# First layer's edge sums: one product of 195 columns per block, with the three parts added on VectorE

## The chip, the cores and the metric

The kernel runs on one core of one Trainium2 chip. The metric is the device time of one execution in microseconds (us). Before the change it is 4831.45 us, the median of 3 runs (4831.15 to 4832.38).

## What is computed

Two layers of a graph transformer over 6250 nodes with 256 features. The change lies in the first layer. Its graph convolution sums, for every node, the projected rows of its neighbours (106,250 directed edges with the loops):

```
x = features * norm_src @ W_gcn                 # 64 columns
agg = segment_sum(x[src], dst, num_segments=n)
h = relu(agg * norm_dst + b_gcn)
x = x + (h @ W_out + b_out) + linear_attention(layernorm(x))
x = x + mixture_of_8_experts(layernorm(x))      # two hidden layers of 256, gates by softmax
```

The second layer has a graph attention, another linear attention, and 4 experts with a router that is itself an attention over 131,072 edges.

## The kernel before

The program runs in stages, one after the other, with a barrier between them. The one that the change touches is the stage of the first layer's experts, class `Stage1`, some 490 to 1958 us into the span. It works on two things that don't need each other until the next tile.

**The experts.** The 49 windows of 128 nodes are taken as 7 tiles of 7 windows. In each tile, 8 experts (`e` 0 to 7) follow one another; expert e of tile c is unit 8c + e. For each unit TensorE makes 4 products of the second hidden layer (`layer(c, e, 1, k)`, L1503), 4 of the next expert's first layer (L1503 again), and 4 `last` products (L1516) for pairs of windows. ScalarE takes the hidden layers out of PSUM (L1645). VectorE adds each `last` result, times the gate, to the rows (`weighted`, L1822).

**The edges of the next tile.** The edges are sorted by destination and cut into blocks of 128 edges, each within one window of destinations. Four blocks are a group (`GROUP = 4`); this stage has 187 groups, q = 0 to 186. GpSimd gathers the rows of a group's source nodes by an indirect DMA for each block (L1392, five buffers of groups). A gathered row is the fp32 value of 65 numbers (64 sums and a count) cut into three bf16 parts, 195 columns in all (`PARTS = 3`, `GCOL = 65`). VectorE makes a 0/1 matrix of destinations for a group (`one_hot`, L1717). TensorE's `edges(q)` multiplies it with the rows: for each of 4 blocks three products of 65 columns, added up in PSUM (L1415, 12 in a group). Two PSUM banks take turns (`q % 2`). VectorE's `add_edges` adds each of the 4 results of 65 columns to the row of its window in `acc` (L1732).

**The order is written out by hand**, and each engine works through its own list. A unit has four places ("shares" 0 to 3) for groups of edges. On TensorE: share 0, a sorting step, `layer` products, share 1, a sorting step, `layer` products, share 2, `last` for pairs 0 and 1, share 3, `last` for pairs 2 and 3, and on to share 0 of the next unit. On VectorE: share 0, share 1, share 2, `weighted` for pairs 0 and 1, share 3, `weighted` for pairs 2 and 3. Most shares hold one group; in the first tile eight of them hold two, and in the units e = 7 shares 1 and 2 follow each other on TensorE with nothing between them.

**Two more things are in VectorE's list.** A bitonic sort of the router's edges, for a later stage, is spread over the units (L1096, L1098, L1112). In 5 units of every tile, and in all 8 of the last, a part of it stands between `weighted` for pair 1 and share 3. TensorE's sorting step turns keys (L1079) and waits for that part (L1163). In e = 1 a bias is added in four steps (L1808), and in e = 7 the next tile's rows are normalised (L1782) and turned by TensorE (L1456).

`edges(q)` waits for the 0/1 matrix, for the rows, and for the adds of group q - 2, that is for its bank. GpSimd waits for the products of group q - 5.

Of the kernel before, what the change touches and what calls it, by code (L numbers as in the profile page):

```python
# [10 lines left out]
ALU = mybir.AluOpType  # L11
ACT = mybir.ActivationFunctionType
AXX = mybir.AxisListType.X
ENG = mybir.EngineType

P = 128
# [15 lines left out]
PARTS = 3  # L32
GCOL = GCN + 1
# [18 lines left out]
GROUP = 4  # L52
# [1118 lines left out]
class Stage1:  # L1171
# [83 lines left out]
    def __init__(self, f, nc, R, A):  # L1255
# [39 lines left out]
        self.gt = f.sb("gt", [E0, TPI, P])  # L1295
        self.h1 = f.sb("h1", [P, C, TOK])
        self.h2 = f.sb("h2", [P, C, TOK])
        self.pe = f.ps("pe", [P, 2, 512])
        self.ph = f.ps("ph", [P, 3, 512])
        self.po = f.ps("po", [P, 2, 2, D])  # L1300
# [2 lines left out]
        self.s_c, self.s_st, self.s_bn, self.s_bnr, self.s_scaled, self.s_made, self.s_cnt = (  # L1303
            f.sem(n) for n in ("c", "st", "bn", "bnr", "scaled", "made", "cnt"))
        self.s_rows = [f.sem(f"rows{b}") for b in range(self.ROWS)]
        self.s_hot, self.s_sum, self.s_acc = (f.sem(n) for n in ("hot", "sum", "acc"))
        self.s_xm, self.s_mixed, self.s_side, self.s_sa, self.s_x = (
            f.sem(n) for n in ("xm", "mixed", "side", "sa", "x"))
        self.s_hf, self.s_nd, self.s_ndr, self.s_hr = (f.sem(n) for n in ("hf", "nd", "ndr", "hr"))
# [87 lines left out]
    def tensor(self, t):  # L1397
# [9 lines left out]
        def edges(q):  # L1407
            b = q % self.ROWS
            t.wait_ge(self.s_hot, q + 1)
            t.wait_ge(self.s_rows[b], 16 * GROUP * (q // self.ROWS + 1))  # L1410
            if q >= 2:
                t.wait_ge(self.s_acc, GROUP * (q - 1))
            for u in range(GROUP):
                for k in range(PARTS):
                    mm = t.matmul(self.pe[:, q % 2, u * GCOL:(u + 1) * GCOL], self.hot[:, q % self.HOTS, :, u],  # L1415
                                  self.rows[:, b, u, k * GCOL:(k + 1) * GCOL], start=(k == 0), stop=(k == PARTS - 1))
            mm.then_inc(self.s_sum, 1)

        def mix(n, q):
# [112 lines left out]
        for c in range(ITER):  # L1532
            more = c + 1 < ITER
            for e in range(E0):
                unit = E0 * c + e
                su = self.sorting(c, e)
                for q in self.share(unit, 0):
                    edges(q)
# [8 lines left out]
                for q in self.share(unit, 1):  # L1547
                    edges(q)
# [9 lines left out]
                for q in self.share(unit, 2):  # L1558
                    edges(q)
# [136 lines left out]
    def vector(self, v):  # L1696
# [13 lines left out]
        def one_hot(q):  # L1710
            if q >= self.GROUPS:
                return
            if q >= self.HOTS:
                v.wait_ge(self.s_sum, q - self.HOTS + 1)
            t = GROUP * (self.first() + q)
            dst = R.gdst[:, t:t + GROUP]
            v.tensor_tensor(self.hot[:, q % self.HOTS], self.count[:, :, :],  # L1717
                            dst.unsqueeze(1).to_broadcast([P, P, GROUP]), ALU.is_equal).then_inc(self.s_hot, 1)

        def add_edges(qs):  # L1720
            for q in qs:
                one_hot(q + self.HOTS - 1)
                t = GROUP * (self.first() + q)
                _, ws = self.nc.values_load_multi_w_load_instructions(
                    R.gwin[0:1, t:t + GROUP], engines=(ENG.DVE,), min_val=0, max_val=W - 1,
                    skip_runtime_bounds_check_because="a count of at most W - 1 windows")
                v.wait_ge(self.s_sum, q + 1)
                for u in range(GROUP):
                    if GROUP * q + u:
                        v.wait_ge(self.s_acc, GROUP * q + u)  # L1730
                    aw = self.acc[:, bass.ds(ws[u], 1), :].rearrange("p a d -> p (a d)")
                    v.tensor_tensor(aw, aw, self.pe[:, q % 2, u * GCOL:(u + 1) * GCOL], ALU.add).then_inc(self.s_acc, 1)  # L1732

        def gather_sums(n, done):
            win[n] = self.windows(ENG.DVE, n)
# [114 lines left out]
        for c in range(ITER):  # L1850
            more = c + 1 < ITER
            for e in range(E0):
                unit = E0 * c + e
                su = self.sorting(c, e)
                add_edges(self.share(unit, 0))
                if e == 0:
                    weigh_gates(c)
# [6 lines left out]
                if su is not None:  # L1864
                    self.sort.vector(v, sst, su, 0)
                add_edges(self.share(unit, 1))
                if e == 1:
                    add_bias(c, 1)
# [4 lines left out]
                if su is not None:  # L1873
                    self.sort.vector(v, sst, su, 1)
                add_edges(self.share(unit, 2))
                if e == 1:
                    add_bias(c, 2)
# [1373 lines left out]
```

## Time and profile before

| | |
|---|---|
| median of 3 runs | 4831.45 us |
| profiled execution | 4826.72 us, of which its span is 4825.0 us |
| PE, busy | 3819.0 us, 79% of the span |
| DVE, busy | 3259.6 us, 68% |
| ACT, busy | 2202.3 us, 46% |
| POOL, busy | 2816.7 us, 58% |

PE is TensorE's matmuls, PEld its weight loads, DVE VectorE, ACT ScalarE, POOL GpSimd. A row of a timeline gives the start in us from the start of the span, the duration, the engine, the line, the operation, what it writes and reads, and its shape. x12 at its end means twelve of a kind in a row. A bracket behind it is the engine's idle time ahead of it and what ended that. The rows of other views end with the busy time, the mean ns of one, and the idle time before them.

### The profile page before, as it was taken

The page shows a single profiled execution, that of the slowest core. Times are in us where ns is not written, and L with a number is a line of the kernel's source. Part 1 is how long each engine was busy: PE and PEld are TensorE (multiplying, and loading weights), DVE is VectorE, ACT ScalarE, POOL GpSimd, SP SyncE. Part 2 cuts the span into 40 slices and gives each one's busy share as a digit, 9 for nine tenths or more (in the row PEclk, how much of TensorE's full clock was granted, in tenths as well). Part 3 has the DMA queues.
Part 4 walks back from the last instruction along what each step waited for, and adds up shares of the span by engine and source line. Part 5 has one row for each costly group of instructions (what it writes and reads, how often), then busy time and mean ns, then how long its engine had stood idle before and what let it go on. Part 6 is the DMA issues. An engine that isn't in the chain of part 4 may idle for free. (4 is left out here: it accounts for less than half of the span.)

```text
span 4825.0 us, 68016 instructions
## 1 busy us (share of the span) xinstructions
PE 3819.0 (79%) x17730; PEld 2381.1 (49%) x17730; DVE 3259.6 (68%) x10150; ACT 2202.3 (46%) x3971; POOL 2816.7 (58%) x2922
## 2 busy tenths in 40 slices
PE   7478789999999999768888888764448888878776
PEld 6344456656665566534444444443424444444444
DVE  7667274645546455488888888876566777777777
ACT  4123222233323223356666666620346666666665
POOL 0355376656656420077777777730477777777775
PEclk9999799999999999989999999886568889998888
DMA  1232311111111100344444444531222222222221
GB/s 60 54 88 64 99 46 34 42 34 37 41 30 40 23 16 1 126 125 138 140 137 136 139 140 140 138 91 32 64 34 39 40 40 44 41 39 40 39 38 28
DMA packets 277159, 323.15 MB, mean 67 GB/s; under 512 B 78502, under 2 KB 232004, under 8 KB 276796
## 3 DMA queue, kind: packets, MB, share of 16 engines
q0 software_dynamic: 105328, 175.77, 16.5%
q1 hardware_dynamic: 171468, 143.20, 10.1%
q8 instruction: 147, 2.41, 0.2%
q14 instruction: 216, 1.77, 0.1%
HBM read 288.85 MB, written 29.89 MB: 66 GB/s over the span
## 5 line engine op out<-in xcount | busy, mean ns | idle before, releaser
L2716 POOL DMA_INDIRECT st_rows<-tabr,router_rsrc x1072 | 1022.2, 954 | 334.7 <-issue 322.1
L1392 POOL DMA_INDIRECT st_rows<-tab,graph_gsrc x748 | 741.8, 992 | 499.8 <-PE st_pe L1415 299.0
L2134 POOL DMA_INDIRECT all_XT<-tab,graph_gsrc x880 | 867.6, 986 | 272.2 <-issue 252.5
L1645 ACT ACTIVATE st_h<-st_ph,st_shift,st_scale 128x448 f32<-128x448 f32 x448 | 324.4, 724 | 757.4 <-PE st_ph L1503 757.2
L2164 PE MATMUL st_po<-all_XT,st_hot 128*128 128x264 f32 x1760 | 579.6, 457 | 84.2 <-DVE gat_sum L2317 83.0
L2317 DVE TENSOR_TENSOR gat_sum<-gat_sum,st_po 128x264 f32 x880 | 376.5, 428 | 143.5 <-DVE gat_sum L2317 75.4
L2164 PEld LDWEIGHTS st_po<-all_XT,st_hot 128*128 128x128 f32 x1760 | 297.5, 204 | 288.1 <-DVE gat_sum L2317 176.3
L2761 PE MATMUL st_px<-all_XT,st_w 128*128 128x512 f32 (+1 forms) x832 | 424.0, 659 | 10.7 <-ACT st_hid L2821 10.7
L1732 DVE TENSOR_TENSOR gcn_acc<-gcn_acc,st_pe 128x65 f32 x748 | 166.3, 222 | 381.7 <-PE st_pe L1415 290.7
L2773 PE MATMUL st_py<-st_w,st_hid 128*128 128x256 f32 x1568 | 422.5, 416 | 0.5 <-ACT st_hid L2821 0.5
L2734 PE MATMUL st_pad<-st_adr,st_hott 128*128 x1072 | 121.1, 183 | 346.4 <-DVE st_zd L2887 325.4
L1516 PE MATMUL st_po<-all_XT,st_h 128*128 128x256 f32 x1568 | 366.7, 385 | 13.5 <-DVE all_X L1822 9.9
L1503 PE MATMUL st_ph<-st_h,all_XT 128*128 128x448 f32 x896 | 363.3, 557 | 3.3 <-ACT st_h L1645 3.3
L1503 PE MATMUL st_ph<-st_xt,all_XT 128*128 128x448 f32 x896 | 361.8, 558 | 0.0
L2773 PEld LDWEIGHTS st_py<-st_w,st_hid 128*128 128x128 f32 x1568 | 305.3, 205 | 44.8 <-ACT st_hid L2821 0.9
L1516 PEld LDWEIGHTS st_po<-all_XT,st_h 128*128 128x128 f32 x1568 | 292.5, 191 | 67.6 <-issue 14.1
L2734 PEld LDWEIGHTS st_pad<-st_adr,st_hott 128*128 128x128 bf16 x1072 | 87.1, 98 | 453.8 <-issue 433.0
L2923 DVE TENSOR_TENSOR router_racc<-router_racc,st_po 128x60 f32 x1072 | 229.8, 214 | 119.9 <-DVE router_racc L2923 6.8
L2810 ACT ACTIVATE st_rows<-st_d 128x16 f32<-128x16 f32 x268 | 57.9, 216 | 509.4 <-DVE st_d L2897 508.4
L2308 DVE TENSOR_TENSOR all_XT<-all_XT,st_wps 128x1024 f32<-128x1024 f32 x220 | 266.8, 1213 | 0.5 <-ACT all_XT L2233 0.5
L1822 DVE SCALAR_TENSOR_TENSOR all_X<-st_po,st_gate,all_X 128x256 f32 x392 | 168.4, 477 | 141.8 <-PE st_po L1516 128.0
L2761 PEld LDWEIGHTS st_px<-all_XT,st_w 128*128 128x128 f32 x832 | 170.9, 222 | 186.2 <-issue 175.2
(489 smaller groups left out, 7233.4 us busy)
## 6 DMA issues: line engine op xcount, KB each, us to landing
st_bc<-drowr SPq DMA_DIRECT2D x268, 128.0 KB
st_bc<-drow SPq DMA_DIRECT2D x220, 128.0 KB
st_rows<-tabr,router_rsrc POOLq DMA_INDIRECT x1072
all_XT<-tab,graph_gsrc POOLq DMA_INDIRECT x880
xtd<-tab_xt SPq DMA_DIRECT2D x98, 128.0 KB, 1.9
st_rows<-tab,graph_gsrc POOLq DMA_INDIRECT x748
tab<-gat_sum SPq DMA_DIRECT2D x7, 924.0 KB
all_XT<-xtd SPq DMA_DIRECT2D x49, 128.0 KB
```

The costliest lines, as they stand in the source:

```text
L1392: g.indirect_dma_start(self.rows[:, b, u, :], None, self.R.tab0, bass.IndirectOffsetOnAxis(self.R.gsrc[:, t:t + 1], 0)).then_inc(self.s_ro ...
L1503: mm = t.matmul(self.ph[:, m % 3, 0:HALF], (self.w1, self.w2)[l][:, e, i, fb * P:(fb + 1) * P], src[:, i, h * HALF:(h + 1) * HALF], start= ...
L1516: mm = t.matmul(self.po[:, q % 2, j - 2 * k, :], self.h2[:, i, j * P:(j + 1) * P], self.wo[:, e, i, :], start=(i == 0), stop=(i == C - 1))
L1645: a.activation((self.h1, self.h2)[l][:, fb, h * HALF:(h + 1) * HALF], self.ph[:, m % 3, 0:HALF], ACT.Relu, bias=self.shift[:, l, i:i + 1], ...
L2134: g.indirect_dma_start(self.rows[:, b, u, :], None, self.R.tab1, bass.IndirectOffsetOnAxis(self.R.gsrc[:, t:t + 1], 0)).then_inc(self.s_ro ...
L2164: t.matmul(self.po[:, m % self.BANKS, 0:GROW], self.hot[:, q % self.HOTF, u], self.rows[:, q % self.ROWS, u, :], start=True, stop=True).th ...
L2308: v.tensor_tensor(m, m, self.wps[:, :, :].unsqueeze(3).to_broadcast([P, GROUP, GH, GC]), ALU.mult)\
L2317: v.tensor_tensor(aw, aw, self.po[:, (GROUP * q + u) % self.BANKS, 0:GROW], ALU.add).then_inc(self.s_acc, 1)
L2716: g.indirect_dma_start(self.rows[:, b, u, :], None, self.R.tabr, bass.IndirectOffsetOnAxis(self.R.rsrc[:, t:t + 1], 0)).then_inc(self.s_ro ...
L2761: mm = t.matmul(self.px[:, i, 0:n * P], self.w1[:, e, c, fb * P:(fb + 1) * P], R.XT[:, c, r * P:(r + n) * P], start=(c == 0), stop=(c == C ...
L2773: t.matmul(self.py[:, m % 2, 0:D], self.hid[:, (E1 * u + e) % 2, fb, j * P:(j + 1) * P], self.w2[:, e, fb, :], start=(fb == 0), stop=False)
L2923: v.tensor_tensor(aw, aw, self.po[:, q % self.SUMB, u * n:(u + 1) * n], ALU.add).then_inc(self.s_acc, 1)
```

## The change

Each block's product is now one of 195 columns instead of three of 65. A block's result takes 195 columns of PSUM, two blocks fill 390 of a bank's 512, and a group fills both banks. So the banks no longer take turns: `edges(q)` waits until the results of group q - 1 have been read. VectorE adds the three parts of each result by two reductions per group (one for each bank), into a new tile `es` in SBUF, and the four adds to `acc` read that tile.

```
+        self.es = f.sb("es", [P, GROUP, GCOL])
@@ edges(q)
-            if q >= 2:
-                t.wait_ge(self.s_acc, GROUP * (q - 1))
+            if q:
+                t.wait_ge(self.s_es, 2 * q)
+            n = PARTS * GCOL
             for u in range(GROUP):
-                for k in range(PARTS):
-                    mm = t.matmul(self.pe[:, q % 2, u * GCOL:(u + 1) * GCOL], self.hot[:, q % self.HOTS, :, u],
-                                  self.rows[:, b, u, k * GCOL:(k + 1) * GCOL], start=(k == 0), stop=(k == PARTS - 1))
+                mm = t.matmul(self.pe[:, u // 2, u % 2 * n:(u % 2 + 1) * n], self.hot[:, q % self.HOTS, :, u],
+                              self.rows[:, b, u, 0:n], start=(u % 2 == 0), stop=False, skip_group_check=True)
             mm.then_inc(self.s_sum, 1)
@@ add_edges(qs)
                 v.wait_ge(self.s_sum, q + 1)
+                if q:
+                    v.wait_ge(self.s_acc, GROUP * q)
+                for h in range(2):
+                    v.tensor_reduce(self.es[:, 2 * h:2 * h + 2, :],
+                                    self.pe[:, h, 0:2 * PARTS * GCOL].rearrange("p (u k d) -> p u d k", u=2, k=PARTS),
+                                    AXX, ALU.add).then_inc(self.s_es, 1)
                 for u in range(GROUP):
+                    v.wait_ge(self.s_es, 2 * q + u // 2 + 1)
                     if GROUP * q + u:
                         v.wait_ge(self.s_acc, GROUP * q + u)
                     aw = self.acc[:, bass.ds(ws[u], 1), :].rearrange("p a d -> p (a d)")
-                    v.tensor_tensor(aw, aw, self.pe[:, q % 2, u * GCOL:(u + 1) * GCOL], ALU.add).then_inc(self.s_acc, 1)
+                    v.tensor_tensor(aw, aw, self.es[:, u, :], ALU.add).then_inc(self.s_acc, 1)
```

## Rows read from the trace of the kernel before

**Rows 1.** The page's part 2: busy tenths and granted clock in 40 slices.

```profile
PE   7478789999999999768888888764448888878776
DVE  7667274645546455488888888876566777777777
PEclk9999799999999999989999999886568889998888
```

**Rows 2.** Windows: us, busy time (x instructions) of each engine, clock, DMA.

```profile
560.00:1760.00 1200.00, 1121.44 (x5818) 732.29 (x5817) 658.88 (x1907) 350.38 (x501) 722.77 (x728) 0.98 0.15 36
```

**Rows 3.** Groups by line, 560 to 1760 us.

```profile
L1732 DVE TENSOR_TENSOR gcn_acc<-gcn_acc,st_pe 128x65 f32 x748 | 166.3, 222 | 381.7 <-PE st_pe L1415 290.7 <-issue 7.6 <-DVE gcn_acc L1732 3.9
L1415 PE MATMUL st_pe<-st_rows,st_hot 128*128 128x65 bf16 x2244 | 103.1, 196 | 11.4 <-DVE gcn_acc L1732 7.9 <-DMA st_rows<-tab,graph_gsrc 2.4 <-issue 1.2
```

**Rows 4.** Timeline of PE in a unit with sorting (shares 2, 3 and 0).

```profile
1100.63 0.56 PE L1415 MATMUL st_pe<-st_rows,st_hot 128*128 128x65 bf16 x12
1101.03 3.70 PE L1516 MATMUL st_po<-all_XT,st_h 128*128 128x256 f32 x16
1104.56 0.56 PE L1415 MATMUL st_pe<-st_rows,st_hot 128*128 128x65 bf16 x12
1107.63 0.56 PE L1415 MATMUL st_pe<-st_rows,st_hot 128*128 128x65 bf16 x12
1109.17 0.63 PE L1079 MATMUL st_side<-all_ident,st_skey 128*128 128x128 f32 x4 [0.98 <-DVEq L1163]
1109.63 6.18 PE L1503 MATMUL st_ph<-st_h,all_XT 128*128 128x448 f32 x16
```

**Rows 5.** Timeline of DVE in the same stretch.

```profile
1102.57 0.68 DVE L1096 TENSOR_TENSOR st_skey<-st_skey 128x512 f32<-128x512 f32 x1
1103.17 0.68 DVE L1098 TENSOR_TENSOR st_skey<-st_skey 128x512 f32<-128x512 f32 x1
1109.70 1.33 DVE L1732 TENSOR_TENSOR gcn_acc<-gcn_acc,st_pe 128x65 f32 x4 [0.17 <-issue]
```

**Rows 6.** Timeline of PE: two bf16 rows of another stage, 256 columns wide.

```profile
4390.80 0.28 PE L2775 MATMUL st_py<-router_b2p,st_ones 3*128 3x256 bf16 x1
4391.01 1.35 PE L2773 MATMUL st_py<-st_w,st_hid 128*128 128x256 f32 x5
```

**Rows 7.** Groups by line, DVE: the later stages' sums of three parts.

```profile
L2290 DVE TENSOR_REDUCE st_zd<-st_pad 128x64 f32<-128x192 f32 x220 | 77.1, 351 | 15.8 <-issue 15.2 <-PE st_pad L2152 0.4
L2887 DVE TENSOR_REDUCE st_zd<-st_pad 128x32 f32<-128x96 f32 x268 | 69.0, 257 | 63.2 <-issue 59.8 <-PE st_pad L2734 3.4
```

**Rows 8.** Timelines of PE and DVE at share 0, first and last late case.

```profile
837.25 0.56 PE L1415 MATMUL st_pe<-st_rows,st_hot 128*128 128x65 bf16 x12
...
837.78 1.32 DVE L1732 TENSOR_TENSOR gcn_acc<-gcn_acc,st_pe 128x65 f32 x4 [0.17 <-issue]
...
1734.24 0.56 PE L1415 MATMUL st_pe<-st_rows,st_hot 128*128 128x65 bf16 x12
...
1735.53 1.32 DVE L1732 TENSOR_TENSOR gcn_acc<-gcn_acc,st_pe 128x65 f32 x4 [0.17 <-issue]
```

**Rows 9.** Timelines of PE and DVE at a share with two groups, first tile.

```profile
635.69 0.96 PE L1415 MATMUL st_pe<-st_rows,st_hot 128*128 128x65 bf16 x24
642.39 0.56 PE L1415 MATMUL st_pe<-st_rows,st_hot 128*128 128x65 bf16 x12 [2.61 <-DVE gcn_acc L1732]
642.79 7.95 PE L1503 MATMUL st_ph<-st_h,all_XT 128*128 128x448 f32 x16
...
640.93 1.32 DVE L1732 TENSOR_TENSOR gcn_acc<-gcn_acc,st_pe 128x65 f32 x4 [0.17 <-issue]
```

**Rows 10.** Timeline of PE: places that already wait for DVE behind its edge adds.

```profile
1029.31 1.77 PE L1425 MATMUL st_side<-st_xm,all_weff 128*128 128x448 f32 x4 [1.13 <-DVE all_X L1808]
...
1172.19 1.06 PE L1456 MATMUL st_side<-all_ident,st_xn 128*128 128x128 f32 x4 [2.50 <-DVE st_xn L1782]
...
1179.49 0.63 PE L1456 MATMUL st_side<-all_ident,st_xn 128*128 128x128 f32 x4 [0.63 <-DVE st_xn L1782]
```

More of the change, by code:

```diff
@@ L1305, in __init__ @@
         self.s_rows = [f.sem(f"rows{b}") for b in range(self.ROWS)]
-        self.s_hot, self.s_sum, self.s_acc = (f.sem(n) for n in ("hot", "sum", "acc"))
+        self.s_hot, self.s_sum, self.s_acc, self.s_es = (f.sem(n) for n in ("hot", "sum", "acc", "es"))
         self.s_xm, self.s_mixed, self.s_side, self.s_sa, self.s_x = (
```

## The prediction, made before the changed kernel was run

> **What bounds the kernel now.** I read the page's slices first. In slices 5 to 16, where the experts of the first layer run, PE stands at 9 tenths or nearly so while DVE stands at 4 to 6, and the granted clock is almost full [rows 1]. The windows view says it in numbers: from 560 to 1760 us, the stretch with edges, PE is busy for 1121 of 1200 us, DVE for 659 [rows 2]. So TensorE bounds this stage, and only 79 us of it are PE's idle time. The stages before and after don't change and follow behind barriers, so what the stage gains or loses the kernel gains or loses. Then the groups by line: the adds of the edges sit behind 291 us of DVE idling for the products, while PE idled only 7.9 us for those adds [rows 3]. VectorE has time on average. The question is whether it has it where TensorE will now wait, and that only the timelines of both engines side by side can tell.
>
> **The product of 195 columns.** A group of 12 products of 65 columns holds PE for 0.40 us: the next work starts 1101.03 - 1100.63 us after it [rows 4], and 24 in a row take 0.96 us against 0.56 for 12 [rows 9]. That is 33 ns for each. The trace has no bf16 product of 128 rows and 195 columns. From below: 16 products of 448 columns in fp32 take 6.18 us, some 375 ns from start to start once the tail of the last is off [rows 4]; taken as two passes over 448 columns that is 0.42 ns per column, so 82 ns for 195 and 0.33 us for a group, 0.07 less than now. From above: the bf16 product of 256 columns is followed 0.21 us later [rows 6], 0.16 us scaled to 195, 0.64 a group, 0.24 more than now. I take 0.07 less, since 65 columns at 33 ns (0.5 ns a column) already lie near the lower price. Over 187 groups that is **-13 us**; the ends are -13 and +45.
>
> The Trainium skill (TensorE: Matmul & The Clock Gate, section Back-to-back issue gap) gives for a stream of weight load and matmul about 81 ns at 128 columns and 131 at 512. Read off between them, as an estimate, 195 columns take 90 ns, and the term would be -7 us instead of -13; the 33 ns measured here at 65 columns lies far under the page's 81.
>
> **The two reductions.** The same kind of sum over three parts from PSUM is in the later stages: 351 ns for 192 elements, 257 for 96 [rows 7], so 0.98 ns an element, and 351 + 198 x 0.98 = 545 ns for 390. Two of a kind that don't depend on each other overlap by 0.08 us (0.68 long, 0.60 apart) [rows 5]: both are done 1.01 us after the first starts, and the first add can start after 0.95. The adds of 65 columns now read SBUF instead of PSUM. I leave them at 222 ns [rows 3]: bounds are 0 and 50 ns gained, the adds being chained by their semaphore (4 in 1.33 us [rows 5], 0.11 between two). So each group costs DVE **0.95 us more**, 178 us in all. DVE then is busy for 837 of some 1300 us, and is still not the bound by its sum. Where DVE idles for a product that costs nothing. The new waits ahead of each add are met before the previous add has ended; nothing.
>
> **The wait that changes.** `edges(q)` waited for the adds of q-2, and now waits for the reductions of q-1. What is queued behind it on TensorE is all the rest: the `last` and `layer` products. The new wait ends 1.01 us plus a semaphore after the moment at which the adds of q-1 start now; between the end of four adds and the start of the PE work that waited for it lie 642.39 - 642.25 = 0.14 us [rows 9]. I used 1.1 us and went through the timelines of all 187 groups: start of L1732 of q-1, plus 1.1, minus start of L1415 of q. In 145 of 186 cases it is negative, mostly by 2 to 7 us, since one `layer` or `last` block lies between. In 41 it is positive, 109 us in all:
> - share 0 of a unit that follows a sorting part: 21 cases of 1.0 to 5.1 us, 61.5 in all. The unit of [rows 4, 5] shows why: PE reaches share 0 at 1107.63, VectorE is in the sort and comes to share 3's adds at 1109.70, so 3.2 us are missing. The first case is 837.78 + 1.1 - 837.25 = 1.6, the last 1735.53 + 1.1 - 1734.24 = 2.4 [rows 8].
> - the first tile, with two groups in a share: 14 cases, 40.2 us. In [rows 9] the second of two groups would start at 636.09; the first one's adds start at 640.93, so PE stands for 5.9 us.
> - e = 7, two groups without work between: 5 cases of 1.4. One case of 0.3 is left.
>
> These are not simply added up. **Share 0:** in 10 of the 21 DVE worked without a pause since share 2, whose own reductions push share 3 by another 0.95; the others had 0.7 us or more of pause to take it up: +11. In 5 cases PE idled right behind share 0 for a sort that will by then be done (0.98 at 1109.17 [rows 4], 8.3 in all), and in two for a bias that comes 1.1 us late instead of the wait's 2.4 and 3.0: -11.5. Sum **61**. **First tile:** the stall at a pair in share 3 is followed by 3.3 us of PE work (second product, two `last`), in which DVE finishes adds, one-hot and the next reductions (2.9 us), so the stall at share 0, old and new, vanishes. With the push, share 0 starts at 640.93 + 0.95 + 1.15 + 3.3 = 646.3 against 642.39 now, 3.9 us late. Unit by unit that gives 2.3, 3.7, 3.9, 3.3, 3.9 and 3.8, and two pairs in share 1 add 2.3 and 1.7: **25**. **e = 7:** the wait for the normalised rows ([rows 10], 2.50) has two groups ahead of it on DVE, and the later one (0.63) one more: 2.85 in 5 tiles, **14**, which takes in the 1.4. **e = 1:** the wait for the bias (1.13 [rows 10]), 6 times 0.95: **6**. Four or five places where PE waits for `weighted` in units without a share 0: **5**. Sum of the stalls: 111 us. PE can't win them back: it has no other slack than its 79 us of idle time, most of which is itself a wait for DVE.
>
> **The clock.** A stop of 2.61 us before 642.39 was followed by 7.95 us for 16 products that take 6.18 at full clock [rows 4, 9]: the clock was at its lower level for a while (1.2 of 2.4 GHz), at a cost of 1.8 us. Of 13 stops of 2.4 to 3.0 us in this stage 9 were followed by such a stretch. The change makes some 20 new stops of 2.4 us or more (15 at share 0, 2 in the first tile, 3 in e = 7). At 0.7 x 20 x 1.8 that is **+25 us**; bounds are 0 and, with every stop paid twice, 70.
>
> The Trainium skill (Perfetto Trace Analysis, section Matmuls) says that independent groups of matmuls should rotate through PSUM banks, so that the evacuation of one lies beside the next one's matmuls. The change gives up just this rotation, and the 2-bank rotation is what lets PE pass the 41 places today (7.9 us of waiting [rows 3]). By that rule it loses, as the sum does.
>
> **The sum**, against the profiled execution of 4826.7 us: -13 + 111 + 25 = +123, so 4949.7. That execution lies 4.7 us under the median of the runs, 4831.45; the forecast is **4954 us** (+2.5%).
>
> **The rivals.**
> *Stalls without the clock* (0.15). For it: 4 of 13 stops of this size left the clock alone. Then 4831.45 - 13 + 111 = 4929.
> *Dearer reductions* (0.14): with 390 elements in steps of 65 the reduction might cost twice the row's price; the rows end at 192 elements. Against it: two widths of the same form lie on one line. One more us per group adds 1 us to the 41 late places and 1 to the pushes and waits (about 26 places), and brings 8 places of share 0 over the edge that now have 0.64 us to spare: +80, 5035.
> *TensorE's work decides, the other side* (0.05). DVE idled 291 us for these very products [rows 3]; if a later start on PE were always made good, because DVE, given the pause, comes ahead, only the 13 us would stay: 4818. It decides from the point at which reductions end before PE comes back, and that needs 2 to 5 us less in DVE's list at share 3. A third of the places would have to be otherwise than the timeline shows. Against it: the list's order is fixed.
> *It nets out* (0.02): the pauses make good most stalls, 4831.
> *The change doesn't do what it says* (0.02): each product of 195 columns at the upper price, with little stalling because PE comes late by itself: 4831.45 + 45 + 60 = 4936.
>
> **How the numbers follow.** The forecast, 0.62, has for its own range 4915 to 4995: stalls of 90 to 130, clock of 0 to 40, product -13 to 0. The first and the last rival lie inside it. The range for 8 in 10 takes half of the way to the dear reductions and something below: 4895 to 5020. A measurement can tell about 0.2% from no change. Faster by more than that: 0.05. Within it: 0.03. Slower: 0.92.
>
> **What the profile after would show.** L1415 as 748 products, a group in 0.33 us from its start to the next work. A new DVE row of 374 reductions, 545 ns each. PE's wait for DVE's reductions at L1415 at some 80 to 100 us, where 7.9 us stood, mostly at share 0 and in the first tile. DVE's idle time for L1415 smaller by over 100 us. A granted clock of the stage under 0.98, with about 14 more dips. All stages behind it as long as before and some 120 us later. Wrong would be: the wait of L1415 under 40 us (then DVE keeps ahead), reductions of 1 us (the dear rival), or a stage behind it that changes its length.

## The result, and the profile after

The changed kernel takes **4964.03 us**, the median of 4 runs (4959.38 to 4965.01), beside 4831.3 us for the kernel before (4825.25 to 4832.38): 1.0275 times as long, with an interval of 1.0259 to 1.0291. That is 132.7 us more; the forecast was 123 more. The profiled execution took 4965.01 us, its span is 4963.3.

The windows view of both kernels is cut into three stretches: the first layer's stage with edges, the stage behind it, the rest. Its columns are those of [rows 2]. Before:

```profile
560.00:1958.00 1398.00, 1315.07 (x6504) 856.89 (x6502) 751.28 (x2107) 410.97 (x588) 722.77 (x728) 0.98 0.13 31
1958.00:3300.00 1342.00, 1045.88 (x3939) 583.63 (x3939) 1094.38 (x2627) 764.34 (x1600) 868.79 (x884) 0.93 0.47 133
3300.00:4825.00 1525.00, 1081.54 (x5064) 675.16 (x5064) 1059.61 (x4485) 867.26 (x1366) 1032.06 (x1084) 0.81 0.22 39
```

And after:

```profile
562.00:2099.00 1537.00, 1348.70 (x5009) 860.57 (x5007) 929.32 (x2481) 410.15 (x588) 714.55 (x728) 0.94 0.14 28
2099.00:3441.00 1342.00, 1046.49 (x3938) 582.62 (x3939) 1095.29 (x2629) 764.17 (x1600) 869.04 (x884) 0.93 0.48 133
3441.00:4963.00 1522.00, 1087.09 (x5064) 677.30 (x5064) 1059.66 (x4482) 866.92 (x1366) 1029.34 (x1084) 0.81 0.24 39
```

The whole loss is in the first row: 1398 us became 1537. PE idled for 1398 - 1315.07 = 82.9 us and now idles for 1537 - 1348.70 = 188.3, so **105 us of the 139 are stops**. PE's busy time grew by 33.6 us although the products became shorter. The granted clock fell from 0.98 to 0.94. (These parts are read from the two profiled executions, which are 138 us apart; the medians are 132.7 apart. A count such as x16 behind an fp32 product counts records, and the trace has two for each: the 16 of 448 columns are 8 products of the kernel.)

Groups by line of the stretch with edges, 560 to 1890 us, which answer to [rows 3]. L1416 is the product, L1732 the reductions, L1740 the adds:

```profile
L1732 DVE TENSOR_REDUCE st_es<-st_pe 128x130 f32<-128x390 f32 x372 | 192.0, 558 | 236.5 <-PE st_pe L1416 233.8
L1740 DVE TENSOR_TENSOR gcn_acc<-gcn_acc,st_es 128x65 f32 x744 | 168.1, 226 | 122.5 <-DVE gcn_acc L1740 122.4
...
L1416 PE MATMUL st_pe<-st_rows,st_hot 128*128 128x195 bf16 x748 | 96.7, 252 | 92.6 <-DVE st_es L1732 92.6
```

A reduction takes 558 ns (545 were forecast), and an add 226. DVE's idle time for the products fell from 290.7 to 233.8 us. The adds wait for each other for 122.4 us. They did so before too: [rows 3] leave 381.7 - 290.7 - 7.6 - 3.9 = 79.5 us of idle time in gaps that are too short for the view to name what ended them. So some 40 us of it are new. PE's wait ahead of the products rose from 7.9 to 92.6 us.

What PE waited for, from 560 to 1890 us (in total, times, longest). After:

```profile
PE st_pe L1416 <- DVE st_es L1732: 92.6, 34, 8.3
PE st_side L1457 <- DVE st_xn L1790: 28.2, 10, 4.0
PE st_po L1517 <- DVE all_X L1830: 19.6, 13, 3.5
PE st_side L1426 <- DVE all_X L1816: 13.1, 6, 2.2
PE st_side L1079 <- DVE all_X L1816: 6.4, 3, 4.0
```

Before, in the same order of meaning apart from the first, which is in [rows 3]; the third row has no counterpart after:

```profile
PE st_side L1456 <- DVE st_xn L1782: 16.1, 10, 2.9
PE st_po L1516 <- DVE all_X L1822: 9.9, 10, 2.4
PE st_side L1079 <- DVEq L1163: 8.5, 7, 2.9
PE st_side L1079 <- DVE all_X L1808: 8.4, 3, 3.0
...
PE st_side L1425 <- DVE all_X L1808: 6.9, 6, 1.3
```

The unit of [rows 4] and [rows 5], with the same groups, lies about 70 us later. Its timelines, PE and then DVE:

```profile
1167.85 0.50 PE L1416 MATMUL st_pe<-st_rows,st_hot 128*128 128x195 bf16 x4
1168.19 3.64 PE L1517 MATMUL st_po<-all_XT,st_h 128*128 128x256 f32 x16
1171.67 0.50 PE L1416 MATMUL st_pe<-st_rows,st_hot 128*128 128x195 bf16 x4
1173.04 2.86 PE L1517 MATMUL st_po<-all_XT,st_h 128*128 128x256 f32 x12 [0.87 <-DVE all_X L1830]
1178.90 0.51 PE L1416 MATMUL st_pe<-st_rows,st_hot 128*128 128x195 bf16 x4 [3.01 <-DVE st_es L1732]
...
1168.39 1.03 DVE L1732 TENSOR_REDUCE st_es<-st_pe 128x130 f32<-128x390 f32 x2 [2.23 <-PE st_pe L1416]
1169.34 0.22 DVE L1740 TENSOR_TENSOR gcn_acc<-gcn_acc,st_es 128x65 f32 x1
1169.77 0.23 DVE L1740 TENSOR_TENSOR gcn_acc<-gcn_acc,st_es 128x65 f32 x1 [0.21 <-DVE gcn_acc L1740]
...
1177.72 1.03 DVE L1732 TENSOR_REDUCE st_es<-st_pe 128x130 f32<-128x390 f32 x2
```

PE has the products of share 3 done at 1172.2 and stands before share 0 for 3.01 us (3.2 were forecast), because DVE comes to the reductions of share 3 only at 1177.72, behind the sort. Ahead of that it already stood for 0.87 us in `last`, for a bank that `weighted` frees. Between 1168.39 and 1178.75 DVE has no pause but the 0.21 us between the adds. The adds start 0.43 us apart (1169.34, 1169.77). Before, four took 1.33 us and each 0.22, so three steps took 1.11 and they were 0.37 apart [rows 3, 5]. Over the whole stage the medians are 0.44 and 0.37.

In the first tile the second of two groups in share 3 waits longest. Here are the products of the first, and the second's behind its wait:

```profile
742.11 0.50 PE L1416 MATMUL st_pe<-st_rows,st_hot 128*128 128x195 bf16 x4
750.95 0.82 PE L1416 MATMUL st_pe<-st_rows,st_hot 128*128 128x195 bf16 x4 [8.34 <-DVE st_es L1732]
```

DVE comes to the first group's reductions only at 749.77. From 730.73 on, at the pair of groups in share 1, it had no pause but those between adds: three groups and their parts of the sort lay ahead.

### The profile page after: what moved, and what is told of

Its sections match the earlier page's. It is cut to its first block and busy times, and to the rows that moved or that the text cites. A ratio compares the mean times of both kernels' runs of the same rounds, so it can differ in the third digit from the quotient of the medians.

```text
span 4963.3 us, 66143 instructions
## 1 busy us (share of the span) xinstructions
PE 3858.2 (78%) x16232; PEld 2385.6 (48%) x16234; DVE 3438.7 (69%) x10524; ACT 2200.7 (44%) x3971; POOL 2805.9 (57%) x2922
## 3 DMA queue, kind: packets, MB, share of 16 engines
q1 hardware_dynamic: 171468, 143.20, 10.1%
## 5 line engine op out<-in xcount | busy, mean ns | idle before, releaser
L1517 PE MATMUL st_po<-all_XT,st_h 128*128 128x256 f32 x1568 | 394.8, 407 | 25.3 <-DVE all_X L1830 21.5
L1732 DVE TENSOR_REDUCE st_es<-st_pe 128x130 f32<-128x390 f32 x374 | 193.1, 558 | 236.5 <-PE st_pe L1416 233.8
L1517 PEld LDWEIGHTS st_po<-all_XT,st_h 128*128 128x128 f32 x1568 | 313.0, 205 | 90.3 <-DVE all_X L1830 27.2
```

The lines of the kernel that those rows point to most:

```text
L1517: mm = t.matmul(self.po[:, q % 2, j - 2 * k, :], self.h2[:, i, j * P:(j + 1) * P], self.wo[:, e, i, :], start=(i == 0), stop=(i == C - 1))
```

## The experiments

The first four experiments ran where the kernel before took 4827.33 us. The other four ran first on another chip, on which the kernel before takes 5737.17 us; these ratios aren't set beside the others, and the same four kernels were run again where it took 4828.64. The row of the windows view under an experiment is that of its first stage, whose end is set 2864.5 us before the end of the span, as in the kernel after. PE's idle time is its length less its busy time.

### The wait alone, in the kernel before

Products, banks and adds are those of before; only `edges(q)` also waits for the adds of group q - 1, up to the third of four.

```
-            if q >= 2:
-                t.wait_ge(self.s_acc, GROUP * (q - 1))
+            if q:
+                t.wait_ge(self.s_acc, GROUP * q - 1)
```

> The kernel before with only the new wait: the products of a group wait for the third add of the group ahead (about 1.0 us after its first add starts, the moment at which the reductions end in the changed kernel). No reductions, 12 narrow products, adds from PSUM. Theory W (TensorE's wait behind VectorE's fixed list makes the loss): VectorE's list is no longer than before, so the pushes by the reductions fall away, but the 41 late places stay: 70 to 75 us of new stops and 25 to 35 us of lower clock behind them, 4925 to 4940 us. Rival D (VectorE's added work makes the loss): within 15 us of the kernel before. PE's wait for gcn_acc at L1415 under W 70 to 90 us, under D under 20.

4917.42 us, ratio 1.0187 (1.0172 to 1.0203): **+90**. The stage and the waits:

```profile
562.00:2052.00 1490.00, 1342.45 (x6501) 870.64 (x6499) 752.66 (x2108) 411.63 (x588) 722.85 (x728) 0.96 0.14 29
...
PE st_pe L1415 <- DVE gcn_acc L1732: 95.7, 34, 6.8
PE st_side L1456 <- DVE st_xn L1782: 10.1, 10, 1.7
PE st_po L1516 <- DVE all_X L1822: 8.0, 7, 2.4
```

The time is below the 4925 to 4940 that were expected. The wait is worth as many us (95.7) as in the kernel after. But PE's idle time is only 147.6 - 82.9 = 65 us longer: while PE stands here, DVE gets ahead, and the other waits shrink (16.1 to 10.1, 9.9 to 8.0, and that for the sort is gone from the view's first rows). 27 us more of busy time come with the lower clock, since no instruction was changed.

### The reductions alone, in the kernel before

Two reductions per group are added on VectorE, with their waits. Each reads the 195 values in the group's own bank twice, so 390 elements as in the kernel after, and 558 ns; their results aren't used. The banks still take turns.

```
+                if q:
+                    v.wait_ge(self.s_acc, GROUP * q)
+                for h in range(2):
+                    v.tensor_reduce(self.es[:, 2 * h:2 * h + 2, :],
+                                    self.pe[:, q % 2, 0:PARTS * GCOL].rearrange("p (k d) -> p d k", k=PARTS)
+                                    .unsqueeze(1).to_broadcast([P, 2, GCOL, PARTS]),
+                                    AXX, ALU.add).then_inc(self.s_es, 1)
                 for u in range(GROUP):
+                    v.wait_ge(self.s_es, 2 * q + u // 2 + 1)
```

> The kernel before with the two reductions of 390 elements per group added on VectorE (their result is used by nobody; they read the group's own PSUM bank), the adds waiting for them as in the changed kernel, while the two banks still take turns and the product is still 12 narrow ones. Theory W: without the new wait the added work of VectorE costs only where TensorE already waited for it (e = 1, e = 7, the first tile): 4855 to 4880 us. Rival D: nearly the whole loss is here, 4940 or more. If the effects simply add up, this one and the run with the wait alone make about the loss of the changed kernel plus 11 us of the product.

4924.88 us, ratio 1.0205 (1.0189 to 1.022): **+98**. Stage, waits and adds:

```profile
562.00:2058.00 1496.00, 1351.70 (x6500) 883.70 (x6498) 924.05 (x2482) 409.27 (x587) 715.77 (x728) 0.95 0.14 29
...
PE st_po L1517 <- DVE all_X L1831: 33.4, 16, 3.8
PE st_side L1457 <- DVE st_xn L1791: 32.2, 10, 4.9
PE st_pe L1416 <- DVE gcn_acc L1741: 15.0, 7, 4.2
PE st_side L1426 <- DVE all_X L1817: 13.0, 6, 2.2
...
1004.66 0.22 DVE L1741 TENSOR_TENSOR gcn_acc<-gcn_acc,st_pe 128x65 f32 x1 [0.21 <-DVE gcn_acc L1741]
1005.09 0.22 DVE L1741 TENSOR_TENSOR gcn_acc<-gcn_acc,st_pe 128x65 f32 x1 [0.21 <-DVE gcn_acc L1741]
```

The time lies between what the two theories gave, 4855 to 4880 and 4940 or more, and this is the run that corrects the theory on record. With the two banks still taking turns, PE waits for the adds 15.0 us only, yet it loses as much as with the wait. It stands at the other places where it needs something that DVE's list makes behind the edges: `weighted`'s banks (33.4, before 9.9), the normalised rows (32.2, before 16.1), the bias. **VectorE's list, busy for 62% of this stage (924 of 1496 us), is a bound of its own once a group costs it 1.15 us more** (2.38 us from its first reduction to the next work, by the median, and 1.24 before).

The two parts alone give 90 + 98 = 188 us. The kernel of the next section has both with the twelve narrow products, and there they cost 148 together (4975.6 - 4827.33). So some 40 us are paid once where either alone would have cost them.

### Twelve narrow products, in the kernel after

The wait, the banks and the reductions are those of after; each block's 195 columns are written by three products of 65.

```
-                mm = t.matmul(self.pe[:, u // 2, u % 2 * n:(u % 2 + 1) * n], self.hot[:, q % self.HOTS, :, u],
-                              self.rows[:, b, u, 0:n], start=(u % 2 == 0), stop=False, skip_group_check=True)
+                for k in range(PARTS):
+                    o = u % 2 * n + k * GCOL
+                    mm = t.matmul(self.pe[:, u // 2, o:o + GCOL], self.hot[:, q % self.HOTS, :, u],
+                                  self.rows[:, b, u, k * GCOL:(k + 1) * GCOL], start=(u % 2 == 0 and k == 0),
+                                  stop=False, skip_group_check=True)
```

> The changed kernel with each block's product as three products of 65 columns into the same 195 columns of PSUM. Everything else as in the changed kernel. My term: a group costs 0.34 us instead of 0.40, so this one is slower than the changed kernel by 7 to 11 us (less than 187 x 0.06 where the time falls into a stop): 4971 to 4975. Rival P (the wide product gains nothing): the same 4964 within 3 us. Rival (wide product gains more, since 12 weight loads stand behind the narrow ones): 20 us slower or more.

4975.6 us, ratio 1.0306 (1.0292 to 1.032), against 1.0275 after: 0.0031 of 4830, so 15 us, or 11.6 between the medians, whose intervals nearly meet. In the traces a group holds PE for 0.34 us with four wide products (1168.19 - 1167.85) and 0.40 with twelve narrow ones, in this run as in [rows 4] (medians 0.344 and 0.401), which is 11 us for 187 groups. The wide product does what it says, and it is a small thing. The stage of this run:

```profile
562.00:2108.00 1546.00, 1360.47 (x6502) 881.47 (x6500) 930.33 (x2482) 411.30 (x588) 713.99 (x728) 0.94 0.14 28
```

Against the kernel before, PE idles for 103 us more and is busy for 45 more with the same products. The wait alone had 65 and 27, the reductions alone 61 and 37. So the some 40 us that are paid once are 24 us of stops and 19 of lower clock in these profiles.

### One wait ahead of the four adds, in the kernel after

The adds waited for their reduction and for the add before. Here the wait for both reductions stands once, ahead of the four.

```
+                v.wait_ge(self.s_es, 2 * q + 2)
                 for u in range(GROUP):
-                    v.wait_ge(self.s_es, 2 * q + u // 2 + 1)
```

> The changed kernel with one wait for both reductions ahead of the four adds instead of one ahead of each add. In the trace of the changed kernel the adds start 0.43 us apart instead of 0.33. Theory: the second wait ahead of each add makes that, so the adds are 0.33 apart again, a group costs VectorE 0.3 us less, and the late places come 0.3 us earlier: 8 to 15 us faster than the changed kernel, 4949 to 4956. Rival: the operand in SBUF makes it; then the distance stays at 0.43 and the time within 3 us of 4964.

4969.52 us, ratio 1.0294 (1.028 to 1.0308): nothing gained, where 8 to 15 us were expected. DVE's timeline in this kernel:

```profile
1020.93 1.03 DVE L1732 TENSOR_REDUCE st_es<-st_pe 128x130 f32<-128x390 f32 x2 [0.53 <-PE st_pe L1416]
1022.11 1.34 DVE L1740 TENSOR_TENSOR gcn_acc<-gcn_acc,st_es 128x65 f32 x4
```

The four adds take 1.34 us again, so they are 0.37 apart as before, and it is the second wait that sets them 0.43 apart. Where they read from has no part in it: the kernel with the reductions alone reads PSUM, and has 0.43 (1004.66, 1005.09). (The expectation took 0.33 for the distance of before: that is 1.33 us divided by four adds, where it has three steps and one add.) But now the first add starts 1.18 us after the first reduction instead of 0.95 (1169.34 - 1168.39), since it needs the second reduction too. The next work starts 2.44 us behind the first reduction, beside 2.40 in the kernel after (1170.79, the next row behind the four adds there, less 1168.39); over all groups the medians are 2.43 and 2.40.

### Share 0 behind the second layer, in the kernel after

TensorE's products of share 0 are moved behind the second of the four `layer(c, e, 1, k)`, in the units e = 0 to 6, so that 4 products of 448 columns (8 records, some 3.2 us) and the sort's turn lie ahead of the wait that stopped PE in 21 units.

```
-                for q in self.share(unit, 0):
-                    edges(q)
+                if e == 7:
+                    for q in self.share(unit, 0):
+                        edges(q)
@@ behind layer(c, e, 1, k)
+                    if k == 1 and e < 7:
+                        for q in self.share(unit, 0):
+                            edges(q)
```

First on the other chip:

> The changed kernel with one thing moved on TensorE: in units e = 0 to 6 the edges of share 0 stand behind the second layer product instead of ahead of the first, some 3 us later; VectorE's list is as it was. Theory W (the stops are a matter of who comes first at share 0): the 20 stops there from the second tile on, 51 us together in the changed kernel, are gone, and with them most of the dips of the clock behind them (15 to 20 times 1.8 us); what remains are the pairs of the first tile and the places that wait for the bias, the rows and the weighted adds. 60 to 85 us faster than the changed kernel, 4880 to 4905. Rival D (VectorE's list as a whole is too long): the stops turn up elsewhere, under 25 us faster, 4940 or more.

5797.42 us there, 1.0115 (1.009 to 1.014) of the kernel before on that chip. Then beside the others:

> The move of share 0 in the changed kernel once more, as the first time fell on a chip on which the kernel before itself takes 5737 us. What was asked there stands: theory W 60 to 85 us faster than the changed kernel of this kind of chip (4880 to 4905 against a kernel before of about 4829), with the 20 stops at share 0 from the second tile on gone; rival D under 25 us.

4951.43 us, ratio 1.0255 (1.0239 to 1.027), against 1.0275: 12.6 us better between the medians, 10 by the ratios, with intervals that overlap. That is far from the 60 to 85 of theory W and within the 25 of its rival. Stage, waits, and the unit shown above:

```profile
562.00:2087.00 1525.00, 1342.67 (x5005) 859.53 (x5003) 930.52 (x2482) 410.68 (x588) 721.74 (x728) 0.94 0.14 28
...
PE st_pe L1416 <- DVE st_es L1736: 51.2, 21, 9.1
...
PE st_po L1517 <- DVE all_X L1834: 26.1, 15, 4.3
PE st_side L1426 <- DVE all_X L1820: 15.0, 6, 4.1
PE st_side L1079 <- DVE all_X L1820: 12.5, 3, 4.5
PE st_side L1437 <- DVEq L1767: 8.8, 4, 2.6
PE st_side L1079 <- DVEq L1163: 8.2, 7, 1.6
...
1179.31 2.86 PE L1517 MATMUL st_po<-all_XT,st_h 128*128 128x256 f32 x12 [1.18 <-DVE all_X L1834]
1183.56 0.63 PE L1079 MATMUL st_side<-all_ident,st_skey 128*128 128x128 f32 x4 [1.40 <-DVEq L1163]
```

The wait at the products fell from 92.6 to 51.2 us, as meant. But PE's idle time fell from 188.3 to 182.3 only. Of the 41 us most came back at the next things that DVE makes late: the sort's turn (8.2, was 0), `weighted` (+6.5), the bias (+1.9 and +6.1), the finished sums (8.8, was 1.7). In the unit shown, 3.01 us at share 0 became 1.40 at the turn, and 0.87 in `last` became 1.18. A stop at a wait is not the cause of itself: PE was ahead of DVE by that much, and it meets DVE again at the next gate.

### The same move in the kernel before

> The kernel before with share 0 moved as in the run with the move in the changed kernel: the control. Two banks take turns here and PE waits only 7.9 us at L1415, so the move should give 0 to 10 us: 4817 to 4828. If it gave 60 us here too, the move would say nothing about the new wait.

5751.15 us on the other chip, 1.0037 (1.0022 to 1.0051) of the kernel before.

> The control once more: share 0 moved in the kernel before. 0 to 10 us faster than it if the move acts on the new wait alone; on the other chip it was 0.4% slower, and if that comes back here, the move has a price of its own of some 10 to 20 us, which belongs to the changed kernel with the move as well.

4830.78 us, ratio 1.0004 (0.9994 to 1.0013). The 0.4% of the other chip didn't come back. The move by itself costs and gives nothing here, so what it does in the kernel after is due to the waits.

### Idle stops filled with useless products

In 15 units whose share 0 waited 2.2 us or more, three fp32 products of 448 columns that nothing reads stand ahead of it.

```
+    FILL = (56, 80, 88, 92, 96, 112, 116, 120, 124, 128, 144, 148, 152, 176, 183)
@@ ahead of share 0
+                if self.share(unit, 0).start in self.FILL and len(self.share(unit, 0)):
+                    t.wait_ge(self.s_g, 8 * unit + 4)
+                    for i in range(3):
+                        t.matmul(self.ph[:, 4 * (2 * unit + 1) % 3, 0:HALF], self.w1[:, 0, 0, 0:P],
+                                 self.w2[:, 0].rearrange("p c d -> p (c d)")[:, 0:HALF], start=True, stop=True)
```

> The changed kernel with three more fp32 products of 448 columns on TensorE, used by nobody, ahead of share 0 in the 15 units where it stands 2.2 us or more there: 2.25 us of work put into a stop of 2.2 to 3.5. They take no time from the path; they only keep the engine at work. Theory C (the clock's dips behind the stops cost about 46 us in all, a third to a half of it behind these 15): 15 to 27 us faster than the changed kernel, 4937 to 4949, and the half-clock time of the stage falls from 171 us by 30 to 50. Rival (the dips come of something else, as of the stage's lower load as a whole): the same time within 4 us, or slower by what the products overshoot.

5757.46 us on the other chip, 1.0036 (1.0022 to 1.0051).

> The three products of no use in 15 of the stops at share 0 once more, for the same reason. Theory C: 15 to 27 us faster than the changed kernel, 4937 to 4949, with 30 to 50 us less of half clock in the stage. Rival: within 4 us of it, or slower.

4953.32 us, ratio 1.0259 (1.0244 to 1.0275); 10.7 us under the median after, with intervals that overlap. Its stage:

```profile
562.00:2087.00 1525.00, 1365.81 (x5095) 871.48 (x5093) 929.57 (x2482) 411.21 (x588) 715.79 (x728) 0.95 0.14 28
```

1537 us became 1525 with more work on PE, and the clock rose from 0.94 to 0.95: in the trace's record of it, the time at the lower clock fell from 172 to 143 us. That is just under the 30 to 50 us less that were expected, and the gain lies between the 15 to 27 of the theory and the 4 of its rival. The filling is only of the share 0 stops, so it can't show the whole of the clock's part.

### All remedies together

The move; in units with two groups in share 3, those adds ahead of the sort's part on VectorE; and the wait for the reductions only ahead of the first and the third add.

```
-                    v.wait_ge(self.s_es, 2 * q + u // 2 + 1)
+                    if u % 2 == 0:
+                        v.wait_ge(self.s_es, 2 * q + u // 2 + 1)
@@ VectorE's unit
-                        add_edges(self.share(unit, 3))
+                        if len(self.share(unit, 3)) < 2:
+                            add_edges(self.share(unit, 3))
@@ behind weighted(c, e, k)
+                    if k == 1 and len(self.share(unit, 3)) > 1:
+                        add_edges(self.share(unit, 3))
```

> The changed kernel with three edits: share 0 moved on TensorE; on VectorE share 3's adds ahead of the sorting part in the units with two groups in that share; and waits for the reductions ahead of the first and third add alone. Theory W: the first gives 60 to 85 us, the second takes the four long stops of the first tile (7.3, 5.8, 7.8 and 8.3 us) down to 1.5 to 2 and gives 20 to 35, the third gives 0.2 us per group where VectorE is late, 3 to 8. 4835 to 4875, so that at best it comes level with the kernel before. Rival D: 4910 or more.

5779.39 us on the other chip, 1.0078 (1.006 to 1.0097).

> All three edits on the changed kernel once more. Theory W: 4835 to 4875, level with the kernel before at best. Rival D: 4910 or more. On the other chip it was 18 us faster than the move alone.

4918.8 us, ratio 1.0185 (1.0171 to 1.0198): 45 us better than after, and still 90 us slower than before. That is rival D's range (4910 or more), not theory W's (4835 to 4875).

```profile
562.00:2053.00 1491.00, 1337.51 (x5007) 856.41 (x5005) 929.74 (x2482) 410.56 (x589) 715.04 (x728) 0.95 0.14 29
...
PE st_pe L1416 <- DVE st_es L1736: 36.4, 19, 6.1
...
DVE gcn_acc L1745 <- DVE gcn_acc L1745: 44.1, 193, 0.6
```

The waits that the view names between adds fell from 122.4 to 44.1 us; with the gaps too short for it, the adds' idle time fell from 123 to 97. PE's wait for the reductions fell to 36.4 us, and the longest stop from 8.3 to 6.1, not to the 2 that was expected. But PE idles for 153.5 us, still 71 more than before. No order of the same work was found here that beats the kernel before.

## Why the prediction was right, and where it was not

**Direction and size.** +132.7 us against +123: right, and inside its own range. The stages behind didn't change (1342 and 1342; 1525 and 1522). The rivals are out, each by its own number: the dear reductions by 558 ns, the stalls without a clock by a clock term of 45 us, that it doesn't do what it says by 0.34 us a group, and the two on TensorE's side by 92.6 us of waiting. One sign was wrong: DVE's idle time for the products was to fall by over 100 us, and fell by 57; the stage that it idles in became 139 us longer.

**The product: right.** 0.34 us a group instead of 0.40, -11 us against -13. One product takes some 84 ns from start to start (the median). The estimate of 90 from the Trainium skill (TensorE: Matmul & The Clock Gate, section Back-to-back issue gap) lies 6 ns above it, the 82 from the rows 2 under it. The 82 rested on taking a record of 375 ns as two passes over its columns; no run tests that by itself.

**The reductions: right alone, wrong with what follows.** 558 ns for 545, the first add 0.95 us after the first reduction, as forecast. "The new waits ahead of each add are met before the previous add has ended; nothing" was **wrong**. They are met, and still cost 0.07 us for each of three steps (0.44 apart for 0.37; the prediction's "0.11 between two" adds was 0.15, by the same slip as above): from the first reduction to the next work a group now takes 2.40 us. Before, it took 1110.94 - 1109.70 = 1.24, by [rows 5] and the row behind it:

```profile
1110.94 1.26 DVE L1822 SCALAR_TENSOR_TENSOR all_X<-st_po,st_gate,all_X 128x256 f32 x3
```

That is 1.16 more and not 0.95: the 0.21 between them are the three steps. In all it is 217 us instead of 178.

**The stalls: the sum right, by parts that offset each other.** 105 us against 111. By part, from the rows of waits and the 34 stops one by one:

| part | forecast | measured |
|---|---|---|
| share 0 | 61 | 50.9 in 21 stops, less the waits for the sort (8.5) and 2.0 at the bias, 40 |
| first tile | 25 | 35.7 in 8 stops, less the 7.9 of before, 28 |
| e = 7 | 14 | 5 stops of 1.22 and 28.2 - 16.1 = 12.1, 18 |
| e = 1 | 6 | 13.1 - 6.9 = 6.2 |
| `weighted` | 5 | 19.6 - 9.9 = 9.7 |

These add up to 102 of the 105 us. The places were right: all 34 stops are among the 41 of the forecast, the 21 of share 0 are its 21, and the 7 that didn't come are 6 of the first tile, each at the next group behind a stop, and the one of 0.3 us. The unit shown has 3.01 us for 3.2. Too much was put on share 0. Its "+11" for the push didn't come: the stops are 50.9 us where the timelines of before gave 61.5, since PE is held up on its way there, in the unit shown by 0.87 us in `last`. What was late once is not late again. At the first tile's pairs in share 3 the stops were longer than the timelines of before gave (7.30 us for 5.9, and 8.34 for 5.0), since DVE, with no pause, reached them later by what each group ahead of them cost more.

**The cause: half right.** The text put the loss on the new wait, with the longer list of DVE as a push of some places, and held "DVE is still not the bound by its sum" to be enough. The wait alone costs 90 us, the reductions alone 98, with the banks still taking turns. Either would have made the change slower by about 2%. By the prediction's own terms the reductions alone were to cost 25 to 50 us (4855 to 4880 in the expectation drawn from it), half of what they did. That its sum came near all the same is in part luck: where both are present, 40 us of the two are paid only once. By its sum DVE has time, 751 and then 929 us of some 1400 to 1540 busy, and yet its list sets the end of PE's waits in the sorting units, since PE takes something from it at several places of each. The prediction held that as a side term, 5 us for `weighted` in "four or five places". Moving share 0 confirmed it: taking 41 us of waiting from the products returned 6 us of idle time. "PE can't win them back" was right. That each stop could be taken away by itself, which the expectation of 60 to 85 us for that run assumed, was not.

The rule of the Trainium skill on rotating PSUM banks (Perfetto Trace Analysis, section Matmuls) held: giving up the rotation alone cost 90 us here. It was not the whole loss.

**The clock: the term mis-sized.** +25 was forecast. Measured, as the growth of PE's busy time in the stage and the gain of the product that hides in it, it is 33.6 + 11 = **45 us**. A second way gives the same: in the trace's record of the clock PE is busy at the lower one for 62.7 us of the stage before and for 152.5 after, and if work takes twice as long there, half of the difference is 45. The size of a dip was nearly right, their number not. The profile has 16 stretches at the lower clock (1.2 of 2.4 GHz) in this stage before and 37 after, 21 more where 14 were forecast, 2.1 us each instead of 1.8. The forecast counted stops of 2.4 us and more at a chance of 0.7. Of stops of 2.35 us or more, 9 of 14 were followed by a lower clock before, but 20 of 23 after; and stops of 2.0 to 2.35 us, of which there had been none, are now 17, of which 10 were followed by it. The forecast had no term for those. Of the 20 new stops of 2.4 us or more that it counted, only 9 to 11 came on balance, by whether the limit is set at 2.35 or 2.40 us; they were followed by the lower clock more often than it assumed, and the shorter ones made up the rest. Seven stretches in either kernel followed no stop of 2 us at once. One of the shorter stops, in the kernel after:

```profile
1870.10 0.51 PE L1416 MATMUL st_pe<-st_rows,st_hot 128*128 128x195 bf16 x4 [2.22 <-DVE st_es L1732]
1870.44 7.90 PE L1504 MATMUL st_ph<-st_h,all_XT 128*128 128x448 f32 x16
```

7.90 us for 16 records of products that take 6.18 at the full clock [rows 4]. Filling 15 of the stops supports this part (12 us off the stage, with PE busier), but doesn't measure all of it.

**What stays open.** How the 40 us shared by the wait and the longer list divide between the sorting units and the first tile was not run. What still holds the best version 90 us above the kernel before is the longer list and what the wait leaves in the first tile, by its rows of waits; no run took either away.

## What to carry to other kernels

An engine that is busy for 62% of a stage can still be a bound of it, if the other engine comes to it several times per unit of a fixed order: price what you add to its list at every such place, not only at the wait that the edit changes. A wait that is moved or hidden gives back little while its maker stays late, because the next gate takes it; a shorter list or a deeper rotation is what is left to try, and no run here tried either. Here four wide products in place of twelve gained 11 us, and the bank rotation and VectorE's sums that they took cost some 145.

## What the runs showed of the hardware that was not expected

- A second semaphore wait ahead of an add that already waits for the one before it sets the adds 0.44 us apart instead of 0.37, although the semaphore had long been raised. It was so with the operand in SBUF and in PSUM, and gone with the wait.
- TensorE's clock fell behind stops as short as 2.0 to 2.35 us in 10 of 17 cases, and in 20 of 23 behind longer ones, where the kernel before had shown 9 of 14.
- Of 37 stretches at the lower clock in the kernel after, 7 had no such stop right ahead of them, as 7 of 16 before; so a stop is not all that precedes a fall.
- One chip of this kind took 5737.17 us for the kernel before, 19% more than the 4828 us measured elsewhere. The two kernels with ratios of 1.0255 and 1.0185 beside 4828.64 us had 1.0115 and 1.0078 there, so a ratio holds for the chip on which it is measured. With share 0 moved in the kernel before, VectorE and ScalarE were busy as long on both (3261 and 2199 us there, 3264 and 2202 here), PE longer (4053 for 3818, at a mean clock of 0.842 for 0.91), and the other 677 of the 912 us are idle time of PE.
